# The second expert stage's row turns: two in three on TensorE, every third by VectorE in blocks of 32

## What is computed

```python
def _L1_ffn_ref(x, Wg, W1, W2):
    B, S, D = x.shape
    E = Wg.shape[1]
    T = B * S
    cap = max(1, T // E)
    xt = x.reshape(T, D)
    logits = xt @ Wg
    probs = jax.nn.softmax(logits, axis=-1)
    ...
    tok2exp = jnp.where(assigned, jnp.argmax(masked, axis=0), jnp.argmax(pT, axis=0))
    weights = jnp.take_along_axis(probs, tok2exp[:, None], axis=1)[:, 0]
    out = jnp.zeros_like(xt)
    for e in range(E):
        gate = jnp.where(tok2exp == e, weights, 0.0)
        h = jax.nn.gelu(xt @ W1[e], approximate=False) @ W2[e]
        out = out + gate[:, None] * h
    return out.reshape(B, S, D)
...
h = _layernorm(x, axis=-1) * (1 + cb) + sb
x = x + gb * _L1_ffn_ref(h, L1_ffn_Wg, L1_ffn_W1, L1_ffn_W2)
```

## Time and profile before

| | us |
|---|---|
| median of 3 runs | 1057.19 |
| range of these | 1055.5 to 1058.59 |
| profiled execution | 1056.4 |
| its span | 1054.5 |
| TensorE busy over the span | 961.7 (91%) |
| VectorE busy over the span | 688.8 (65%) |

### The profile page before, as it was taken

How to read it: one execution, slowest core, us unless ns; L and a number is a source line. 1 busy time by engine, 2 the same in 40 slices (tenths; PEclk the granted TensorE clock), 3 DMA queues, 4 the chain that set the end, 5 groups by cost and what they waited for, 6 DMA issues and landing times. The chain is left out here.

```text
span 1054.5 us, 30361 instructions
## 1 busy us (share of the span) xinstructions
PE 961.7 (91%) x11177; PEld 825.1 (78%) x11178; DVE 688.8 (65%) x1736; ACT 495.4 (47%) x1343; POOL 386.0 (37%) x341
## 2 busy tenths in 40 slices
PE   6999999989999999999978999999767889999996
PEld 3466666889999999999866777778656878899995
DVE  3478877856777777777504688888985777344442
ACT  2656665304445545544346787777552440322221
POOL 0435334521332232231204555555561101455552
PEclk9999999999999999999998999999958999999998
DMA  9775571394322222221065655766421620444441
GB/s 338 231 313 125 120 263 41 116 376 111 99 79 90 97 81 88 91 92 59 22 112 84 127 111 138 148 132 129 92 67 53 249 124 19 153 133 139 133 135 35
DMA packets 133009, 135.59 MB, mean 129 GB/s; under 512 B 73868, under 2 KB 122126, under 8 KB 130724
## 3 DMA queue, kind: packets, MB, share of 16 engines
q1 hardware_dynamic: 121668, 90.80, 31.0%
q0 software_dynamic: 11232, 43.27, 12.9%
HBM read 96.21 MB, written 44.77 MB: 134 GB/s over the span
## 5 line engine op out<-in xcount | busy, mean ns | idle before, releaser
L1146 PE MATMUL psall<-rows 128*128 128x128 f32 x1872 | 223.6, 276 | 1.4 <-DVE rows L1232 1.4
L1146 PEld LDWEIGHTS psall<-rows 128*128 128x128 f32 x1872 | 218.4, 193 | 2.9 <-issue 1.8
L1109 POOL DMA_INDIRECT x<-ffn_rows,tok_i x78 | 82.1, 1053 | 172.1 <-DVE tok_i L994 90.6
L1160 PE MATMUL psall<-whi,rows 128*128 x624 | 141.0, 379 | 0.0
L1232 DVE COPY rows<-wlo 128x2048 f32 (+2 forms) x78 | 74.1, 950 | 94.7 <-PE psall L1146 85.8
L1160 PEld LDWEIGHTS psall<-whi,rows 128*128 128x128 f32 x624 | 115.7, 190 | 14.1
L1114 POOL DMA_INDIRECT attn_rows<-rows,tok_i x39 | 42.0, 1077 | 183.3 <-DVE rows L1264 183.3
L1492 DVE STREAM_TRANSPOSE whi<-whi 32x512 f32<-32x512 f32 x128 | 89.8, 701 | 9.0 <-POOL whi L1455 7.7
L279 PE MATMUL psall<-cst 128*128 128x128 f32 x714 | 89.9, 283 | 0.5 <-PEq L1375 0.5
L1572 ACT ACTIVATE whi<-psall 32x512 f32<-32x512 f32 x128 | 75.1, 587 | 30.3 <-PE psall L1701 27.3
L1294 ACT ACTIVATE rows<-psall,vs 128x128 f32<-128x128 f32 x312 | 84.7, 382 | 9.5 <-PE psall L1146 7.1
(11 more groups left out here) (256 smaller groups left out, 1738.5 us busy)
## 6 DMA issues: line engine op xcount, KB each, us to landing
ffn_rows<-mod_rows SPq DMA_DIRECT2D x2, 4096.0 KB
wlo<-in_W SPq DMA_DIRECT2D x2, 4096.0 KB, 17.5
whi<-in_w SPq DMA_DIRECT2D x5, 1024.0 KB, 8.4
whi<-mod_rows SPq DMA_DIRECT2D x4, 1024.0 KB, 15.2
ffn_rows<-rows SPq DMA_DIRECT2D x8, 512.0 KB
ffn_rows<-x SPq DMA_DIRECT2D x8, 512.0 KB
wlo<-attn_rows SPq DMA_DIRECT2D x32, 128.0 KB, 3.4
v_turn<-wlo SPq DMA_DIRECT2D x32, 128.0 KB, 2.7
```

Source lines behind the costliest of these rows:

```text
L1109: eng.indirect_dma_start(xin[j % DEEP], None, src_d, bass.IndirectOffsetOnAxis(tok_i[:, j:j + 1].bitcast(U32), 0), bounds_check=T, oob_is_ ...
L1146: last = eng.matmul(b_up[t.par][f // 4][:, (f % 4) * P:(f % 4 + 1) * P], w_now[:, c, f * P:(f + 1) * P], inT[t.par][:, c * P:(c + 1) * P], ...
L1160: last = eng.matmul(b_dn[t.par][:, 0:D], hidT[t.par][:, f * P:(f + 1) * P], w_down[:, bass.ds(e, 1), f, :].rearrange("p o n -> p (o n)"), ...
```

## The change

In the second layer's experts, every third tile (t mod 3 = 2, from tile 5 on, so 5, 8, ..., 38, twelve of them) is no longer turned on TensorE but by VectorE in blocks of 32, eight instructions in step t and eight in step t + 1, into one of two buffers. For that the other stages of the second layer now lag two steps more on every engine, as in the first (`ahead` = 2). ScalarE's `act_in` waits for the signal tb and reads from SBUF for these tiles. The first layer keeps its pattern (`every` = 2).

```diff
@@
+                self.in_three, self.threes, self.three_slot = at % 3, i * (DEEP // 3) + at // 3, at // 3 % 2
...
-            def by_blocks(self):
+            def by_blocks(self, every):
-                return self.par == 1 and self.after(3)
+                return self.par == 1 and self.after(3) if every == 2 else self.in_three == 2 and self.after(5)
...
-            ahead = 2 if normed else 0
+            ahead, every = 2, 2 if normed else 3
...
                 def turn_in(t):
-                    if normed and t.by_blocks():
+                    if t.by_blocks(every):
                         return
                     eng.wait_ge(s_in[t.slot], (t.rounds + 1 + rounds_before[t.slot]) * 16)
                     if t.after(1):
-                        eng.wait_ge(e_["inT"], t.j - 1 if normed and t.after(3) else t.j)
+                        eng.wait_ge(e_["inT"], t.j - 1 if t.after(4) and (normed or t.in_three == 0) else t.j)
...
                 def act_in(t):
                     e = expert_of(eng, t)
-                    blocks_in = normed and t.by_blocks()
+                    blocks_in = t.by_blocks(every)
                     if blocks_in:
-                        eng.wait_ge(e_["tb"], t.pairs)
+                        eng.wait_ge(e_["tb"], t.pairs if normed else t.threes)
                     elif normed and t.after(2):
                         eng.wait_ge(e_["tin"], t.pairs + 2)
+                    elif not normed and t.after(3):
+                        eng.wait_ge(e_["tin"], t.threes * 2 + 2 + t.in_three)
...
                 def turn_blocks(half):
                     def stage(t):
-                        if not t.by_blocks():
+                        if not t.by_blocks(every):
                             return
                         if half == 0:
                             eng.wait_ge(s_in[t.slot], (t.rounds + 1 + rounds_before[t.slot]) * 16)
-                            if t.after(7):
+                            if t.after(7 if normed else 11):
                                 eng.wait_ge(e_["inT"], t.j - 5)
-                        to = turned[t.odd_slot].rearrange("p (c i t) -> p c i t", c=C, i=4)
+                        to = turned[t.odd_slot if normed else t.three_slot].rearrange("p (c i t) -> p c i t", c=C, i=4)
...
-                    pipeline(eng, [(0, fetch_weights), (2, out_rows)], head)
+                    pipeline(eng, [(ahead, fetch_weights), (0, turn_blocks(0)), (1, turn_blocks(1)), (ahead + 2, out_rows)], head)
```

More of the change, by code:

```diff
@@ L1087, in expert_stage @@
             nbank = nf * P // 512
-            names = "tin inT w half up act dn y sum" + (" tb b bs mv ln rs out" if normed else "")
+            names = "tin tb inT w half up act dn y sum" + (" b bs mv ln rs out" if normed else "")
             e_ = {n: sem(f"{tag}_{n}") for n in names.split()}
@@ L1181, in act_in @@
                     settle(eng)
-                    prep_in(eng, e, inT[t.par], turned[t.odd_slot] if blocks_in else b_in).then_inc(e_["inT"], 1)
+                    prep_in(eng, e, inT[t.par], turned[t.odd_slot if normed else t.three_slot] if blocks_in else b_in).then_inc(e_["inT"], 1)
                 def act_hidden(t):
```

## The result

The changed kernel takes 1065.9 us in the median of 6 runs (1063.9 to 1067.0), the kernel before 1056.2 beside it. The ratio is 1.0084, with a 95% interval of 1.0067 to 1.0101: slower by 9 us by the ratio and by 9.7 us by the two medians. 1065.5 us was forecast, 9.1 more than the profiled execution before. The profiled execution took 1066.5 us, its span 1064.4 against 1054.5.

A forecast was written before the change was run, and what follows sets the result against it. TensorE was taken to bound the second expert stage; after the change a 12.03 us gather circle replaces 11.205 us per three tiles, 11 times +0.83: 1056.4 + 9.1 = 1065.5 us, range 1058.5 to 1071.

The forecast's parts named there:

- What a saved turn is worth: TensorE, second expert stage: each turn removed saves 0.215 us, twelve turns -2.6 us, as long as nothing else is late.
- The size of the transposes: VectorE: eight 32x64 transposes take 1.99 us, 236 ns each, as in the first stage; 3.98 us a tile.
- Rival 2: VectorE: a half takes under 1.28 us, every step stays under 3.52; whole -2.6 us comes in, 1053.8; chance 0.05.
- The gap to the next copy: VectorE's queue from L1251's start to the next weight copy: 0.90 us taken, 1.26 as upper end.
- The step with a half: VectorE's step with copy, eight transposes, row products, sums and queue work: 4.23 us, over TensorE's 3.735.
- The circle: Gather landing, transposes, sums, next gather: 12.03 us against TensorE's 11.205 for three tiles; +0.83 each, 11 times, +9.1 us.
- the branch: Loop's branch on VectorE, every second triple: some 0.36 us late by VectorE's steps alone, nothing in the circle.
- A steps: VectorE's steps with the first half of a turn; their transposes wait about 0.8 us for the gather.
- triples: Three tiles, three VectorE steps: first half of a turn, second half, none; 12.0 us forecast instead of 11.2.
- rival 1: The gather is hidden, VectorE's step length alone decides: 1.0 plus about 1.8 for branches, +2.8 us, 1059.2; chance 0.13.
- C's copy: Weight copy in VectorE's step without transposes: starts 1.41 us after the up products (bound 1.11), TensorE waits 0.30.
- Priced at nothing: Two steps of lag, ScalarE's read from SBUF (0.39 us, covered) and GpSimd's issues: all 0 us.

The follow-up runs named there:

- e2: Changed kernel with half of the transposes left out (four in each half turn instead of eight), waits kept: ratio 0.9990 to the kernel before.
- e10: Changed kernel, second stage written out, row products first, transposes 6, 5, 5 over three steps, seven row and three output buffers: ratio 0.9998 to the kernel before.
- e5: Changed kernel with the second stage's steps written out, so no loop and no branch: ratio 1.0105 to the kernel before, 12.13 us for three tiles.
- e1: Changed kernel turning a constant region instead of the gathered rows, without VectorE's wait for the gather (wrong data): 1060.7 us, ratio 1.0046 to the kernel before.
- e6: Changed kernel with the second stage written out and eight row buffers instead of six: 1056.4 us, ratio 0.9994 to the kernel before.
- e3: Changed kernel with every second-stage tile turned on TensorE as before, only the two steps of lag kept: ratio 1.0010 to the kernel before.
- e9: Changed kernel, second stage written out, seven row buffers instead of six and three output buffers instead of two: ratio 1.0035 to the kernel before.
- e4: Changed kernel with row products and sums before the half turn in each VectorE step: 1060.1 us, ratio 1.0041 to the kernel before.

## Why the prediction was right, step by step

**What a saved turn is worth.** 0.215 us: e2 and e10 run three tiles in 10.98 us against 11.20 before.

**The size of the transposes.** Eight in 1.98 to 1.99 us, 236 ns each, in this stage too: the row of the first stage carried over. The Trainium skill's 311 ns for a 128x128 of bf16 ("VectorE: DVE Perf Modes", section "The three transpose paths") did not carry over to this form, float32 in sixteen instructions, which takes 3.97 us for two squares. Rival 2, which needed under 1.28 us for a half, fell with it.

**The gap to the next copy.** 0.90 us from L1251's start was chosen, 1.26 kept as upper bound: measured 0.91 (959.21 to 960.12). The step with a half came to 4.17 us instead of 4.23, since the row products follow the transposes in some 0.03 us and not in 0.10.

**The circle.** The sum was 12.03 us; the stage ran at 12.00, and e5, without the branch, at 12.13. By terms, from the rows above: transposes 1.98 and 1.99, each time 0.53 or 0.55 to the sums' start (0.62 taken, with the 0.10), 0.91 to the copy, 0.73 from there, 0.42 and 0.78 to the gather, 3.94 to its landing: 11.83 of the 11.85 us between the two A steps shown. Where the chain has the gathers of other triples they took 4.04 to 4.48 us, and the median of the stage is 4.3 instead of 4.0; this and the shorter steps cancelled. That the gather is part of it, e1, e5 and e6 show. The +9.1 us and the measured 9 to 9.7 rest on the same mechanism, with some luck in these two terms.

**Who waits in which triple.** Here the prediction was not quite right. It had every A after the first wait 0.8 us for the gather; eight of these eleven do, for 0.75 in the mean. Triples with the loop's branch in them take 4.17 us, then 4.58 to 4.76, then 3.00, so up to 11.93 by VectorE's steps alone. That is almost the circle's length, and the wait ahead of the next A is nothing or 0.16 us. The sum hardly changed by it: e5, in which all eleven wait, runs at 12.13 and not at 12.00.

**The mis-sized term: rival 1.** VectorE's steps alone were priced at +2.8 us; e1 measured 1.0046, some +5. Two parts of its sum were short. From C's copy to A's its terms give 0.69 + 0.14 + 1.79 + 0.20 = 2.82; it is 3.00 (0.75 + 2.05 + 0.20), because the up products take longer after TensorE has waited (last section). And the branch costs 0.41 to 0.59 instead of 0.36. The rows named for that 0.36 give more themselves: the load of tile_expert starts 0.55 us after L1251 in one and 0.06 in the other, so 0.49 apart. So the added VectorE work, without any gather, makes half of the loss. The time alone could not have told the two apart: e1's 1060.7 us lies within the forecast's range of 1058.5 to 1071 too, and it took e1, e5 and e6 to show the circle.

**Priced at nothing.** The lags and the loop's place (e3) are nothing. ScalarE's read from SBUF takes 0.42 us and stays covered, but for one wait of 0.5 us near the end of the stage. GpSimd's issues are no limit (busy 28.48 of 50 us), but they grew, and the landings in the circle with them (last section).

## What to carry to other kernels

Work moved from a full engine to a half idle one has to fit into the idle engine's window in each step, not into its mean: here 2 us in a step of 3.7 with 1.6 us of other work and 0.5 of queue work did not fit, 1.2 to 1.5 us did. Before a stage is moved earlier in a software pipeline, count the steps between what frees its buffer and what reads it, and close the circle with the DMA's latency. If it is longer than the steps, it sets the pace. One buffer more (e9) or two (e6) took the wait for the gather away here. The order within a step counts too: with the row products ahead of the transposes (e4), the gather was released earlier and the queue's register work ran beside the transposes, but VectorE then waited for the down products. That gave about half of the loss back.

## What the runs showed of the hardware

TensorE needs longer for a series after a wait. In the chain of the changed kernel, the up products that waited for the weight copy:

```profile
940.85 0.71 DVE rows L1235
941.60 2.05 PE psall L1147 x16
943.65 1.74 PE psall L1161 x8
```

2.05 us against 1.79 in a series without a pause: a wait costs some 0.26 us beyond the idle time shown. In the timeline of TensorE the series itself lasts 2.05 us after a wait and 1.95 without one, which is 0.10 of it; the other 0.16 is that its start no longer overlaps the products before. A VectorE queue in a hardware loop needs 0.48 us from the sums to the next copy and 0.87 to 1.07 where the loop's branch lies between, against 0.38 when the steps are written out. GpSimd's issue of a gather took 1.31 us in the median of the changed kernel instead of 1.02, and the landings 4.3 us instead of 4.0 in the median. A landing is counted from the start of its issue, and 4.3 - 1.31 and 4.0 - 1.02 both leave 3.0: in the medians the whole difference is the issue, and what follows it takes as long as before. In e4_rows_first, which does as many transposes at other times, the issue took 1.02 and the landings 4.0 again. What VectorE's and GpSimd's work share there was not tried.
